# A decoder layer on one core: an attention output projection in three float32r passes, its parts formed from the PSUM bank, and split chunks loaded in place

## The reference

```python
qh = _split_heads(jnp.einsum('bnq,qi->bni', x, Wq))
kh = _split_heads(jnp.einsum('bmc,ci->bmi', context, Wk))
vh = _split_heads(jnp.einsum('bmc,ci->bmi', context, Wv))
sim = jnp.einsum('hid,hjd->hij', qh, kh) * SCALE
mean = jnp.mean(sim, axis=-1, keepdims=True)
sim = (sim - mean) * ATTN_MATRIX_SCALE + mean
attn = jax.nn.softmax(sim, axis=-1)
out = jnp.einsum('hij,hjd->hid', attn, vh)
...
return jnp.einsum('bni,iq->bnq', out, Wout) + bout
```

## Time and profile before

| | before |
|---|---|
| median of 3 runs | 1330.17 us (1330.01 to 1332.84) |
| the profiled execution: its own time / its span | 1332.3 us / 1330.2 us |
| granted TensorE clock, mean | 0.990 of full speed |
| PE busy | 1287.7 us, 97% |
| DVE busy | 1023.5 us, 77% |
| ACT busy | 895.9 us, 67% |
| POOL busy | 907.9 us, 68% |

### The profile page before, as it was taken

The page is one execution under the profiler, slowest core; times in us unless marked ns, Lnnn a source line. Parts: engine busy times, 40 slices in busy tenths (PEclk is TensorE's granted clock), DMA queues, the critical chain, the costliest instruction groups (busy, mean ns, idle before and its releaser), DMA issues. The chain is left out here.

```text
span 1330.2 us, 22729 instructions
## 1 busy us (share of the span) xinstructions
PE 1287.7 (97%) x8358; PEld 1077.1 (81%) x8358; DVE 1023.5 (77%) x1628; ACT 895.9 (67%) x1315; POOL 907.9 (68%) x645
## 2 busy tenths in 40 slices
PE   5999999999999999999999999999999999988998
PEld 4688888888887788888888888888888888777998
DVE  6355498759317889999999999999999899985554
ACT  4555433425655878878778778778787777775774
POOL 2544410225410899989989999999999989863553
PEclk9999999999999999999999999999999999997999
DMA  6703032246764989988888888888888888796672
GB/s 219 104 6 74 4 101 81 67 130 245 208 233 140 247 213 231 221 196 216 215 203 215 216 201 218 215 196 221 214 201 217 201 191 208 185 252 244 203 230 76
DMA packets 172377, 241.35 MB, mean 181 GB/s; under 512 B 34179, under 2 KB 78085, under 8 KB 172272
## 3 DMA queue, kind: packets, MB, share of 16 engines
q1 hardware_dynamic: 155040, 208.11, 62.0%
q10 hardware_dynamic: 15184, 25.96, 5.7%
q0 software_dynamic: 2048, 5.90, 1.1%
HBM read 64.79 MB, written 41.32 MB: 80 GB/s over the span
## 5 line engine op out<-in xcount | busy, mean ns | idle before, releaser
L1217 POOL TENSOR_TENSOR xa_pT<-xa_moved,xa_pT 128x1024 fp32r<-128x1024 f32 x246 | 589.0, 2428 | 27.1 <-ACT xa_pT L1735 26.0
L1557 PE MATMUL xa_S<-xa_kT,xa_qT 128*128 128x512 f32 x1536 | 389.1, 401 | 1.2 <-ACT xa_probs L1741 1.2
L1741 ACT ACTIVATE xa_probs<-xa_S,xa_mx_nb_rinv 128x1024 f32<-128x1024 f32 x256 | 285.9, 1117 | 146.8 <-DVE xa_mx_nb_rinv L1339 146.8
L1574 PE MATMUL xa_O<-xa_pT,xa_v 128*128 128x512 f32 x1536 | 377.2, 394 | 2.9 <-DVE xa_pT L1392 2.6
L1336 DVE TENSOR_REDUCE xa_mx_nb_rinv<-xa_S 128x1 f32<-128x1024 f32 x256 | 305.3, 1211 | 78.1 <-PE xa_S L1557 78.0
L1574 PEld LDWEIGHTS xa_O<-xa_pT,xa_v 128*128 128x128 f32 x1536 | 289.0, 189 | 69.9 <-DVE xa_pT L1392 2.9
L1557 PEld LDWEIGHTS xa_S<-xa_kT,xa_qT 128*128 128x128 f32 x1536 | 288.5, 188 | 67.9 <-ACT xa_probs L1741 2.9
L1349 DVE STREAM_TRANSPOSE xa_tq<-xa_probs 128x1024 f32<-128x1024 f32 x256 | 316.7, 1238 | 15.0 <-ACT xa_probs L1741 7.3
L1735 ACT ACTIVATE xa_pT<-xa_moved 128x1024 fp32r<-128x1024 f32 x254 | 253.9, 1050 | 2.1 <-PE xa_O L1574 1.1
L506 PE MATMUL fw_pp<-fw_hT,fw_wqk 128*128 128x512 f32 x384 | 95.0, 405 | 4.3 <-DVE fw_hT L647 4.3
L506 PEld LDWEIGHTS fw_pp<-fw_hT,fw_wqk 128*128 128x128 f32 x384 | 73.4, 194 | 20.7 <-DVE fw_hT L647 3.0
(11 more groups left out here) (247 smaller groups left out, 1679.1 us busy)
## 6 DMA issues: line engine op xcount, KB each, us to landing
xa_moved<-xa_tq SPq DMA_DIRECT2D x508, 256.0 KB, 4.5
heads_k<-ci_outs SPq DMA_DIRECT2D x32, 256.0 KB, 2.0
heads_v<-ci_outs SPq DMA_DIRECT2D x32, 256.0 KB, 2.3
heads_q<-ci_outs SPq DMA_DIRECT2D x32, 256.0 KB, 2.4
xa_chunk<-heads_v ACTq DMA_DIRECT2D x32, 256.0 KB, 4.2
ex_w1s<-in_L_ffn_w_dram SPq DMA_DIRECT2D x8, 1024.0 KB, 7.3
ex_w2s<-in_L_ffn_w_dram SPq DMA_DIRECT2D x8, 1024.0 KB, 9.7
xa_chunk<-heads_q ACTq DMA_DIRECT2D x31, 256.0 KB, 4.2
```

The source lines that it names most:

```text
L1217: pool.tensor_tensor(quadrants(pT[LO], r), unit_moved(r), quadrants(pT[HI], r).bitcast(F32), ALU.subtract).then_inc(lo_ready, 1)
L1557: last = pe.matmul(banks[:, k % 2], qT[a][:, i // GT % 2, q], kT[b][h % 2][:, k * 512:(k + 1) * 512], start=(n == 0), stop=(n == 2))
L1574: last = pe.matmul(O[:], v[a][:, j * P:(j + 1) * P], pT[b][:, r % PRING, k], start=(j == 0 and n == 0), stop=(j == JT - 1 and n == 2))
L1741: act.activation(probs[:, unit % RING], S[:, score_banks(unit)].rearrange("p a b -> p (a b)"), ACT.Exp, bias=nb[:, s % 2:s % 2 + 1], scale ...
```

## The change: the projection of groups 0 to 27 in three passes, and a new plan of chunks

- `out_project` of the first 28 groups (heads 0 to 6, `SPLIT_GROUPS`) uses three float32r passes for each of its products in place of one float32 product. Groups 28 to 31 stay as they were.
- For this `copy_oT` writes the high part `oTs[HI]` from the bank O, and a new step on DVE, `output_low`, subtracts it from the same bank into `oTs[LO]`. The bank is free for the next group only after that: PE's wait ahead of the next group's first matmul is on `out_lo` in place of `oT_ready`.
- `copy_oT` moves on ACT from the start of slot 4g+11 to slot 4g+10, behind the exponentials and ahead of the chunk; `output_low` stands on DVE at the start of slot 4g+11.
- The weights `woh` are split too: a new chunk "w" of 128 x 256 in slot 2 of head 0 and in slot i=11 of heads 1 to 6. `out_project(4h, 0)` waits for its low part.
- Chunks of q, k, v are loaded straight into the place of their low part and split there; the ring is gone. The load for slot s+1 is issued in slot s, behind the chunk of slot s, and holds the waits for the old contents of that place.
- The chunks stand in other slots: before at i = 0 to 10 and 13, now at 0, 1, 3 to 8 and 10 to 14 (w among them).
- SP loads `woh` at i=0 in place of i=7; POOL's `constants` and one DVE step wait for the last three-pass projection, since they reuse its memory.

```diff
+        SPLIT_GROUPS = SLOTS // GT - 4
+        def group_of_outputs(s):
+            g, phase = divmod(s - LAG - GT, GT)
+            return g if phase == 0 and 0 <= g < SPLIT_GROUPS else None
...
-            plan = {0: ("k", h + 1, 0), 1: ("q", h, 1), 2: ("k", h + 1, 1), 3: ("k", h + 1, 2), 4: ("v", h, 0),
-                    5: ("q", h, 2), 6: ("v", h, 1), 7: ("v", h, 2), 8: ("v", h, 3), 9: ("k", h + 1, 3),
-                    10: ("q", h, 3), 13: ("q", h + 1, 0)}
+            plan = {0: ("k", h + 1, 0), 1: ("q", h, 1), 3: ("k", h + 1, 1), 4: ("q", h, 2), 5: ("v", h, 0), 6: ("v", h, 1),
+                    7: ("v", h, 2), 8: ("v", h, 3), 10: ("q", h, 3), 11: ("w", h, 0), 12: ("k", h + 1, 2),
+                    13: ("q", h + 1, 0), 14: ("k", h + 1, 3)}
...
+            def output_low(g):
+                dve.wait_ge(oT_ready, g + 1)
+                if g:
+                    dve.wait_ge(y_mm, 2 * g)
+                dve.tensor_tensor(by_tile(oTs[LO][:]), by_quadrant(O[:]), by_tile(oTs[HI][:]).bitcast(F32),
+                                  ALU.subtract).then_inc(out_lo, 1)
...
             for s in range(END):
+                g = group_of_outputs(s)
+                if g is not None:
+                    output_low(g)
                 if s < SLOTS:
                     maxima(s)
...
-                if q == 0 and g:
+                if q == 0 and 0 < g <= SPLIT_GROUPS:
+                    pe.wait_ge(out_lo, g)
+                elif q == 0 and g:
                     pe.wait_ge(oT_ready, g)
...
-                if k == 0:
+                if k == 0 and g < SPLIT_GROUPS:
+                    pe.wait_ge(chunk_lo, place["w", g // 4, 0] + 1)
+                    pe.wait_ge(out_lo, g + 1)
+                elif k == 0:
                     pe.wait_ge(oT_ready, g + 1)
                     pe.wait_ge(wo_in, 16 * (g // 4 + 1))
...
-                    t = 2 * k + m
-                    last = pe.matmul(output_bank(g, k)[:, m], oT[:, t * P:(t + 1) * P], woh[:], start=True, stop=True)
+                    t = slice((2 * k + m) * P, (2 * k + m + 1) * P)
+                    if g < SPLIT_GROUPS:
+                        for n, (a, b) in enumerate(PARTS):
+                            last = pe.matmul(output_bank(g, k)[:, m], oTs[a][:, t], wohs[b][:], start=(n == 0), stop=(n == 2))
+                    else:
+                        last = pe.matmul(output_bank(g, k)[:, m], oT[:, t], woh[:], start=True, stop=True)
...
+                if group_of_outputs(s + 1) is not None:
+                    copy_oT(group_of_outputs(s + 1))
                 if s < SLOTS:
                     for c in chunks_of(s):
                         chunk_high(c)
+                    for c in chunks_of(s + 1) if s + 1 < SLOTS else ():
+                        if c[0] != "w":
+                            load(place[c])
```

More of the change, by code:

```diff
@@ L904, in cross_block @@
         first_in = [sem(f"xa_first_in{i}") for i in range(FIRST)]
-        chunk_in = [sem(f"xa_chunk_in{i}") for i in range(CRING)]
+        chunk_in = sem("xa_chunk_in")
         chunk_hi, chunk_lo = sem("xa_chunk_hi"), sem("xa_chunk_lo")
@@ L1063, in staged @@
                 return moved[:].rearrange("p r q j n -> p (r q j n)")[:, n * UNIT:(n + 1) * UNIT]
-            return chunk[:, n % CRING]
+            kind, h, part = order[n]
+            cols = slice(part * UNIT, (part + 1) * UNIT)
+            if kind == "k":
+                return raw_k[h % 2][:, cols]
+            if kind == "w":
+                return woh[:]
+            return raw_v[:, cols] if kind == "v" else raw_q[:, part % 2]
         def target(c, a):
@@ L1147, in _ @@
                 h, i = divmod(p, TILES)
-                if h and i == 7:
-                    sp.wait_ge(y_mm, 8 * h)
+                if h and i == 0:
+                    sp.wait_ge(chunk_lo, place["w", h - 1, 0] + 1)
                     sp.dma_start(woh[:], w_out[h * XD:(h + 1) * XD, :]).then_inc(wo_in, 16)
@@ L1205, in chunk_low @@
                 n = place[c]
-                kind, h, part = c
-                if kind == "v" and h == 0:
-                    for u in range(UNITS - OUTS, UNITS):
-                        if u % OUTS == part + 1:
-                            written(pool, u)
                 pool.wait_ge(chunk_hi, n + 1)
@@ L1232, in constants @@
             def constants():
-                pool.wait_ge(chunk_lo, len(order))
+                pool.wait_ge(y_mm, 2 * SPLIT_GROUPS)
                 pool.memset(ones[:], 1.0).then_inc(consts, 1)
@@ L1377, in row_stats @@
                 if m == 0:
-                    dve.wait_ge(chunk_lo, len(order))
+                    dve.wait_ge(y_mm, 2 * SPLIT_GROUPS)
                 for i in range(2):
@@ L1701, in load @@
             def load(n):
-                if n - CRING >= FIRST:
-                    act.wait_ge(chunk_lo, n - CRING + 1)
-                for u in units_of(order[n]):
+                c = kind, h, part = order[n]
+                if kind == "k" and h >= 2:
+                    act.wait_ge(sim_done, 2 * TILES * (h - 1))
+                if kind == "q" and 4 * h + part >= 2:
+                    act.wait_ge(sim_done, 2 * GT * (4 * h + part - 1))
+                if kind == "v" and h == 0:
+                    for u in range(UNITS - OUTS, UNITS):
+                        if u % OUTS == part + 1 or part == QUADS - 1 and u % OUTS == 0:
+                            written(act, u)
+                if kind == "v" and h:
+                    act.wait_ge(pv_done, 2 * (TILES * h - GT + part) + 2)
+                for u in units_of(c):
                     written(act, u)
-                act.dma_start(chunk[:, n % CRING], source(order[n])).then_inc(chunk_in[n % CRING], 16)
+                act.dma_start(staged(n), source(c)).then_inc(chunk_in, 16)
             def chunk_high(c):
@@ L1712, in chunk_high @@
                     act.wait_ge(first_in[n], 16)
-                else:
-                    act.wait_ge(chunk_in[n % CRING], 16 * ((n - FIRST) // CRING + 1))
-                if kind == "k" and h >= 2:
-                    act.wait_ge(sim_done, 2 * TILES * (h - 1))
-                if kind == "q" and 4 * h + part >= 2:
-                    act.wait_ge(sim_done, 2 * GT * (4 * h + part - 1))
-                if kind == "v" and h == 0 and part == QUADS - 1:
-                    for u in range(UNITS - OUTS, UNITS):
-                        if u % OUTS == 0:
-                            written(act, u)
-                if kind == "v" and h:
-                    act.wait_ge(pv_done, 2 * (TILES * h - GT + part) + 2)
+                elif kind == "w":
+                    act.wait_ge(wo_in, 16 * (h + 1))
+                    if h:
+                        act.wait_ge(y_mm, 8 * h)
+                else:
+                    act.wait_ge(chunk_in, 16 * (loaded.index(n) + 1))
                 act.activation(target(c, HI), staged(n), ACT.Copy).then_inc(chunk_hi, 1)
-                if FIRST + CRING <= n + 1 < len(order):
-                    load(n + 1)
             def high_part(r):
@@ L1785, in _ @@
                 copy_out(n)
-            for n in range(FIRST, FIRST + CRING):
-                load(n)
             act.wait_ge(w_lo, 2)
```

36 lines of the change are left out of this document (26 added, 10 removed).

## The result

The changed kernel takes 1354.49 us (median of 4 runs, 1352.27 to 1357.96), the kernel before, timed beside it, 1330.09 us (4 runs, 1329.42 to 1332.84). The ratio is 1.0182, with a 95% interval of 1.0153 to 1.021: 24.4 us slower. The forecast was 1360 us, its range 1334 to 1374.

The account below looks back on a forecast made before the run. PE, busy 97% of the span, was taken as the bound, so its added waits count in full. The terms -7 + 12.4 + 20.4 + 4 = +29.8 us on 1330.2 gave 1360 us; bounds 1350 to 1372, widened for rivals to 1334 to 1374.

Parts of the forecast that it names:

- three passes: Projection on PE: six passes take 0.75 us against 0.87 a pair; 0.12 us gained over 56 pairs, -7 us.
- wait for O: PE's first load into O waits for DVE's subtraction: 0.46 us in 27 groups, +12.4 us, bounds +10 to +21.
- wait for w: First projection of heads 1 to 6 waits for POOL's low part of w: 3.4 us six times, +20.4 us.
- clock: PE's clock halves after two or three of the six w waits, about 1.7 us each: +4 us, bounds 0 and +10.
- chunks in the stream: Spreading q, k, v chunks over the head costs nothing and can give back 1.8 us at most.
- all four bounds (-10): Lower bounds relative to the terms: -3 passes, -2.4 wait for O, -0.6 wait for w, -4 clock; range starts at 1350.
- two of three (+12): Upper bounds +8.6 wait for O, +3.3 wait for w, +6 clock, at most two together; range ends at 1372.
- The rival that weight loads bound the passes: Each pass takes as long as a present weight load: +23 in place of -7, 1390 us; chance 0.03.
- What costs nothing: DMAs, POOL's added work, spread chunks, ACT's w chunks, waits moved to ACT's loads, groups 28 to 31: no cost.
- The waits moved to ACT's loads are over when ACT comes to them: ACT's loads, behind its exponentials, find scores or O of the slot before already done: no cost.
- The wait that pays once: A PE stall's lead is kept, so only the first waits for O and w cost: 1327 us; chance 0.07.
- The two rivals with one wait hidden: Wait for w hidden, O's stays: 1336 us, chance 0.08; wait for O hidden, w's stays: 1348 us, chance 0.08.

Follow-up runs that it names:

- float32 in their place: Changed kernel with w chunk and O's low part both sooner, each three-pass product replaced by one float32 product of high parts: 1332.75 us, ratio 1.0001 to before.
- PE kept busy: Changed kernel plus 12 dummy float32 matmuls into Y's bank ahead of the wait for w in heads 1 to 6: 1351.37 us, ratio 1.0153 to before.
- plan alone: Changed kernel with no group split, all float32 projections, no w chunk; loading in place and new chunk slots stay: 1331.98 us, ratio 1.0004 to before.
- both: Changed kernel with the w chunk one slot sooner and O's copy and subtraction moved sooner: 1323.38 us, ratio 0.9932 to before.
- low part of O sooner: Changed kernel with O's copy between slot 4g+10's exponentials and the subtraction ahead of its last transpose: 1354.62 us, ratio 1.0168 to before.
- the subtraction twice: Changed kernel with the w chunk one slot sooner, plus DVE's subtraction done twice: 1352.94 us, ratio 1.0152 to before.

## Why the prediction was right, step by step

**The mechanism.** Right for everything that it had in the sum: two waits, their releasers, their counts, none for w in head 0, the order in POOL that makes w late. The forecast was +29.8 us; the stream gave +25.9 and the medians +24.4. One thing that it put at nothing, ACT's loads in head 0, was not nothing (below).

| term | forecast us | measured us | by |
|---|---|---|---|
| three passes, 54 pairs | -7 | -8.6 | float32 in their place |
| wait for O | +12.4 | +8.6 | 27 x 0.32, by its removal |
| wait for w | +20.4 | +20.2 | 6 x 3.37; -27.3 with its clock |
| clock | +4 | +6.9 | PE kept busy |
| chunks in the stream | 0 | -1.4 | plan alone |
| sum | +29.8 | +25.7 | stream: +25.9 |

The sum is nearer than its terms: wait for O, passes and chunks came out 6.8 us lower than forecast in all, the clock 2.9 higher, and that much of the agreement is luck. So is the size of the clock's term, as shown below. The range was not added up evenly either: its lower end takes all four bounds (-10), its upper end two of three (+12).

**The passes.** Forecast 0.12 us a pair, measured 0.16. The weight loads of a pair in the changed kernel (from 687 us, slot 47):

```profile
687.01 2.59 PEld L1613 LDWEIGHTS xa_O<-xa_pT,xa_v 128*128 128x128 f32 x12 [0.50 <-DVE xa_oT_lo L1426]
689.64 0.41 PEld L1634 LDWEIGHTS xa_Y<-xa_wouts,xa_oT_hi 128*128 128x128 f32 x2
689.98 0.19 PEld L1634 LDWEIGHTS xa_Y<-xa_wouts,xa_oT_lo 128*128 128x128 f32 x1
690.10 0.31 PEld L1634 LDWEIGHTS xa_Y<-xa_wouts,xa_oT_hi 128*128 128x128 f32 x2
690.34 0.19 PEld L1634 LDWEIGHTS xa_Y<-xa_wouts,xa_oT_lo 128*128 128x128 f32 x1
690.46 1.71 PEld L1594 LDWEIGHTS xa_S<-xa_kT,xa_qT 128*128 128x128 f32 x8
```

From load to load it is 0.12 us inside the pair (689.98 to 690.10), near the 0.124 of the experts' rows. From its first load to the next scores it is 0.82 us, not 0.75, because the first gap is that of the 512-column matmul ahead of it; but the scores in turn get their second load 0.12 us behind their first in place of 0.22, so the pair saves 0.05 + 0.10 = 0.15 us. I had counted the pair and not what stands at its borders. The rival that weight loads bound the passes is refuted by the same rows.

By the Trainium skill ("TensorE: Matmul & The Clock Gate", section "Back-to-back issue gap", the rule for an isolated matmul) a pass would be 109 ns and the gain, as an estimate, 12 us; the loads inside the pair stand 120 ns apart, so the trace does not agree, and the measured 8.6 us lies between my term and that rule's.

**The wait for O.** This is the term that was mis-sized: "PE's load is at +0.46 in place of 0: 0.46 us a group". The place is right. DVE's line took 654 ns on the mean (forecast 692), group of 450 to 1180 us:

```profile
L1426 DVE TENSOR_TENSOR xa_oT_lo<-xa_O,xa_oT_hi 128x512 fp32r<-128x512 f32 x28 | 18.3, 654 | 0.4 <-ACT xa_oT_hi L1797 0.4
```

The idle time before the load is 0.49 to 0.50 us, 0.44 more than the spacing of before. But after it PE gains a part back: from its first load into O to the projection it is 2.63 us (687.01 to 689.64) where the earlier trace rows have 2.74. The load that follows the waiting one comes after 0.11 us in place of 0.23 (the first two loads, each 0.19 us long; timeline of PEld in 656.25 to 656.4 us before and 687.0 to 687.3 us after):

```profile
656.07 0.42 PEld L1574 LDWEIGHTS xa_O<-xa_pT,xa_v 128*128 128x128 f32 x2
...
687.01 0.30 PEld L1613 LDWEIGHTS xa_O<-xa_pT,xa_v 128*128 128x128 f32 x2 [0.50 <-DVE xa_oT_lo L1426]
```

What remains is 0.33 us by these rows. Taking the wait away gave 8.65 us of stream, 0.32 for each of the 27. The bound of 10 us that the prediction set from below was too high for the same reason.

**The wait for w.** Forecast 3.4 us six times; the idle times are 3.51 us and cost 3.37 each net of the same effect. ACT's high part took 0.41 us (forecast 0.38), POOL's low part:

```profile
L1239 POOL TENSOR_TENSOR xa_wouts<-xa_wout,xa_wouts 128x256 fp32r<-128x256 f32 x6 | 4.4, 740 | 0.0
```

740 ns against 0.77 forecast.

**The clock.** "Two or three of the six waits" was right, three; "at half clock 3.3 us of PE time cost about 1.7 us" was too small, since two of the three stretches were twice as long. The windows of the changed kernel:

```profile
562.00:568.70 6.70, 6.01 (x17) 5.04 (x18) 1.22 (x1) 1.64 (x2) 5.34 (x3) 0.50 0.76 178
...
664.40:667.70 3.30, 3.30 (x11) 2.91 (x12) 0.00 (x0) 0.83 (x1) 3.30 (x2) 0.50 0.82 119
667.80:1060.20 392.40, 380.40 (x1718) 308.19 (x1716) 358.10 (x464) 303.99 (x450) 362.25 (x178) 1.00 0.83 204
1060.40:1067.10 6.70, 5.63 (x16) 4.75 (x17) 1.23 (x1) 2.00 (x3) 5.72 (x4) 0.50 0.77 181
```

0.50 is 1.2 GHz, 1.00 is 2.4. In the stretch of 392 us that is full throughout lie three more of the waits, which did not cost the clock. The kernel with PE kept busy puts the price at 6.9 us.

That the number three came out is in part luck, for the length of an idle time does not settle what the clock does. The program of the first block is the same in all nine kernels, and the idle times in their profiled executions can be compared. Those of 2.79 or 2.80 us ahead of the matmuls at about 28 us left the clock full in five executions; in the other four it was 2.93 or 2.94 us, and the clock fell each time. Of the later idle time, ahead of the same 14 small matmuls, 2.21 us cost the clock in "both" and did not in "low part of O sooner" (windows over these idle times' ends):

```profile
45.60:48.90 3.30, 2.81 (x19) 2.33 (x20) 1.97 (x4) 0.24 (x1) 2.70 (x8) 0.50 1.17 137
...
44.00:52.00 8.00, 5.79 (x40) 4.75 (x38) 2.22 (x6) 4.13 (x7) 7.62 (x18) 1.00 0.89 112
```

The prediction had one execution of each idle time to count from.

**What costs nothing.** The spread of the chunks was right for the stream: a gain of 1.4 us within the 1.8 allowed. "The waits moved to ACT's loads are over when ACT comes to them" failed in head 0. The changed kernel has the same stall as the plan alone, shorter:

```profile
432.34 2.01 ACT L1782 ACTIVATE xa_pT<-xa_moved 128x1024 fp32r<-128x1024 f32 x2 [1.50 <-DMA heads_q<-ci_outs]
```

ACT's queue stands at the load of a v chunk until that store has landed. Slots 0 to 12 take 1.2 us more than before in the changed kernel and 1.6 to 3.1 more in the seven others. In most of them the loss goes with the length of this stall: 1.2 us at 1.5, 1.6 at 2.0, 1.8 at 2.2, 2.5 at 2.8, 3.1 at 3.4 (the last also has a stretch at half clock there). No experiment moved this load alone, so that it is the cause of those microseconds is read from the rows, not shown.

**The rivals.** The wait that pays once is refuted by the subtraction twice. The two rivals with one wait hidden became kernels: 1332.9 us where the forecast of that case said 1336, and 1354.6 where it said 1348, the latter since the clock and the w wait took back what the wait for O gave. What stays open is why the clock fell in three waits and not in the other three: I read one execution of each kernel, and of the others only the mean clock is on record.

## What to carry to other kernels

Where one engine is busy all the time, a helper's result that it needs has a date, and the cost of the change is that date minus the one at which it is asked for, times how often; read both from the timeline before trading arithmetic for extra passes. The position of one small chunk, one slot too late, cost 20 us by its wait and, in the execution read, some 7 by the clock, about three times the 8.6 us that the passes gave; with the chunk a slot sooner and the subtraction 1.2 us sooner the same change is 0.7% faster than before. And two waits of one slot are not independent: remove the one that ends last first.

## What was not expected of the hardware

- A wait at a weight load costs less than its idle time shows. After waits of 0.49 to 0.50 us the next load followed in 0.11 us in place of 0.23, and a wait of 0.44 us over the usual spacing cost 0.32 us. (Inside the pair of three-pass products, too, the loads stand 0.12 us apart, and 0.23 between 512-column matmuls.)
- With idle times of about 3.5 us at its weight loads, among dense matmuls, PE lost the full clock in three of six cases, and with idle times of 3.9 us in five of six; the stretches at 1.2 GHz were 3.3 or 6.7 us long. 24 small matmuls in the idle time kept it at 2.4 GHz all six times. The length of an idle time alone does not decide: 2.21 us ahead of the same matmuls cost the clock in one execution and not in another. The Trainium skill says in "TensorE: Matmul & The Clock Gate", section "What's actually happening", that the throttled state is the default and activity releases it; these six agree, and which of the waits without such matmuls lose the clock the rule by itself does not say.
